# A state-space stage on one core: a gate copy, router scores and a residual placed later, and each convolution half made in two parts

## The reference

```
h  = layernorm(x) * (1 + ca) + sa
xs, z = split(h @ W_in.T)                       # 256 + 256 columns
xc = silu(conv over 4 rows (xs) + conv_b)       # one filter of 4 taps a column
dt, B, C = split(xc @ W_x.T, [64, 80])
dt = softplus(dt @ W_dt.T + b_dt)
h_t = exp(dt * A) * h_(t-1) + dt * B * xc       # 256 columns x 16 states
y  = sum over the 16 states of h * C, + D * xc
x  = x + ga * ((y * silu(z)) @ W_out.T)
h  = layernorm(x) * (1 + cb) + sb               # goes on to the router of the experts
```

## Time and profile before

| | us |
|---|---|
| median of 3 runs | 663.12 |
| the three runs | 655.6, 663.12, 663.97 |
| the profiled execution | 653.8 |
| its span in the trace | 651.7 |
| the loop over 64 steps, from the first scan to the last sum | about 32 to 277.5 |

### The profile page before, as it was taken

How to read it: one execution, slowest core, us unless ns; L and a number is a source line. 1 busy time by engine, 2 the same in 40 slices (tenths; PEclk the granted TensorE clock), 3 DMA queues, 4 the chain that set the end, 5 groups by cost and what they waited for, 6 DMA issues and landing times.

```text
span 651.7 us, 9201 instructions
## 1 busy us (share of the span) xinstructions
PE 511.0 (78%) x2287; PEld 314.1 (48%) x2287; DVE 454.8 (70%) x870; ACT 335.0 (51%) x667; POOL 426.0 (65%) x324
## 2 busy tenths in 40 slices
PE   8879969979997898977998882659887787847420
PEld 4324323423443333455998871225655676746320
DVE  5877989898989799874445531836780686668717
ACT  3757734674677354342333331563741787737605
POOL 2376989898899879703777775510107778777540
PEclk9779979997998968997999996998887899869675
DMA  6423335433223333012655553500026655452025
GB/s 200 129 77 122 134 129 172 138 102 115 97 97 108 115 89 112 13 41 85 184 182 169 159 139 97 197 2 0 17 76 189 209 165 162 131 134 87 32 86 140
DMA packets 47798, 75.47 MB, mean 116 GB/s; under 512 B 6434, under 2 KB 23716, under 8 KB 47620
## 3 DMA queue, kind: packets, MB, share of 16 engines
q1 hardware_dynamic: 42180, 63.48, 31.2%
q0 software_dynamic: 5568, 11.41, 6.7%
HBM read 65.76 MB, written 9.11 MB: 115 GB/s over the span
## 4 chain that ended last, share of the span: by engine, by line
PE 45%; DVE 18%; issue 10%; ACT 9%; POOL 7%; DMA 6%; DVEq 5%; SPq 1%; POOLq 0%
PE ps L1201 14%; PE ps L1164 4%; PE ps L1195 4%; DVE hs L1863 4%; DVEq L1929 4%; POOL y_dram L487 3%; PE ps L1509 3%; PE ps L1537 3%; PE ps L1400 3%; POOL xl L481 3%; DMA y_dram<-ys,rows_i 2%; PE ps L1108 2%; DVE freq L2070 1%; ACT ps L723 1%; DVE prod L1873 1%
## 5 line engine op out<-in xcount | busy, mean ns | idle before, releaser
L533 POOL TENSOR_TENSOR bu<-uT,b_sb 128x1024 f32<-128x1024 f32 x62 | 145.9, 2374 | 2.1 <-DMA b_sb<-b_rows 2.1
L1201 PE MATMUL ps<-prod,cst 128*128 128x512 f32 x256 | 130.2, 653 | 3.2 <-DVE yT L1883 3.2
L481 POOL DMA_INDIRECT xl<-h_dram,rows_i x87 | 87.6, 1007 | 62.0 <-DVE rows_i L1742 36.1
L487 POOL DMA_INDIRECT y_dram<-ys,rows_i x87 | 94.7, 1088 | 33.7 <-issue 23.5
L723 ACT ACTIVATE ps<-dtT,neg_a 128x512 f32<-128x512 f32 x128 | 85.2, 684 | 53.9 <-DVE hs L1863 53.5
L544 POOL TENSOR_TENSOR prod<-hs,c_sb 128x1024 f32<-128x1024 f32 x32 | 76.6, 2393 | 23.5 <-PE ps L1201 14.8
L1201 PEld LDWEIGHTS ps<-prod,cst 128*128 128x128 f32 x256 | 50.1, 206 | 82.8 <-issue 78.0
L1863 DVE TENSOR_TENSOR_SCAN hs<-ps,carry,bu 128x512 f32<-128x512 f32 x64 | 77.5, 1261 | 4.5 <-ACT ps L723 4.5
L1863 DVE TENSOR_TENSOR_SCAN hs<-ps,bu 128x512 f32<-128x512 f32 x64 | 73.9, 1203 | 7.3 <-ACT ps L723 7.1
L1509 PE MATMUL ps<-xt,mfr 128*128 128x128 f32 x384 | 56.3, 303 | 25.3 <-DVE freq L2062 15.9
L1509 PEld LDWEIGHTS ps<-xt,mfr 128*128 128x128 f32 x384 | 52.2, 215 | 28.1 <-issue 27.1
(11 more groups left out here) (289 smaller groups left out, 834.5 us busy)
## 6 DMA issues: line engine op xcount, KB each, us to landing
b_sb<-b_rows SPq DMA_DIRECT2D x31, 512.0 KB
mfr<-in_mf SPq DMA_DIRECT2D x48, 256.0 KB, 3.4
w1r<-in_w SPq DMA_DIRECT2D x39, 256.0 KB
c_sb<-b_rows SPq DMA_DIRECT2D x32, 256.0 KB, 3.5
w_s<-in_w SPq DMA_DIRECT2D x9, 256.0 KB, 3.9
h_dram<-h_tok SPq DMA_DIRECT2D x8, 256.0 KB
down_s<-in_down SPq DMA_DIRECT2D x1, 2048.0 KB, 9.9
xl<-h_dram,rows_i POOLq DMA_INDIRECT x87, 3.6
```

The lines of the kernel that those rows point to most:

```text
L481: pool.indirect_dma_start(xl[:, j % slots, :], None, h_dram[l], bass.IndirectOffsetOnAxis(ap=rows_i[:, 0, j:j + 1], axis=0)).then_inc(load ...
L487: pool.indirect_dma_start(y_dram[l], bass.IndirectOffsetOnAxis(ap=rows_i[:, 1, j:j + 1], axis=0), ys[:, j % XR, :], None).then_inc(saved[j ...
L533: nc.gpsimd.tensor_tensor(bu[:, g % RING, :, :], uT[:, c % 2, :, :], b_sb[:, k % BRING, g % 2, :].unsqueeze(1).broadcast_to([P, ND, CHUNK] ...
L1201: last = nc.tensor.matmul(bank(Y_BANK + d), ident, prod[:, g % RING, d, :], start=n == 0, stop=n == NS - 1)
```

## The change

The change has five parts. (1) PE: a convolution half no longer makes its four taps at once. Two stand where the four stood, then come the row of C and the sum of the even step, and then the other two; `conv_ps` is raised after the fourth. (2) ACT: the gate's second copy moves from n = 15 to n = 0 of the next chunk, behind the decays of that chunk's state 1. (3) DVE: the router scores are taken at n = 3 and not at 1, the residual is added at n = 7 and not at 6, its inverse deviation made at n = 10 and not at 9. (4) ACT: `rstd` at n = 9 and not at 8. (5) PE: 8 matmuls of `spin` ahead of the wait for the last chunk's columns, before the loop.

```diff
--- before.py
+++ after.py
@@ -757,8 +757,8 @@
                 nc.scalar.activation(ws[:, :, :, :].rearrange("p k b e -> p (k b e)"), src, ACT.Copy).then_inc(S["small_ready"], 1)
 
             before = {2: lambda c: conv_copy(c, 0), 4: lambda c: conv_copy(c, 1), 7: low_and_rows, 9: lambda c: dt_parts(c, 0),
-                      11: lambda c: dt_logs(c, 1), 13: lambda c: z_copy(c, 0), 15: lambda c: z_copy(c, 1)}
-            after = {8: lambda c: rstd(1, c), 12: normed_rows, 14: columns_out}
+                      11: lambda c: dt_logs(c, 1), 13: lambda c: z_copy(c, 0)}
+            after = {9: lambda c: rstd(1, c), 12: normed_rows, 14: columns_out}
             def mod_rows(lb):
 
                 m, src = mod[:, lb // BATCH, lb % BATCH, :, :], bank(MODB[lb]).rearrange("p (k c) -> p k c", c=C)
@@ -802,6 +802,8 @@
                     scaled_scores(vec[:, V["rw0"]], modT0, wq0)
                 if g == 6:
                     centred_scores(2, ps[:, BACK, 0:2 * BATCH * E0], ws0)
+                if n == 0 and c:
+                    z_copy(c, 1)
                 if n in before and c + 1 < NCHUNK:
                     before[n](c + 1)
                 if n == 5:
@@ -1153,17 +1155,19 @@
                 nc.tensor.matmul(bank(z_bank(c, d)), win_s[:, DIN + d * P:DIN + (d + 1) * P], hT[:, b, lo:lo + CHUNK],
                                  start=True, stop=True).then_inc(S["z_ps"], 1)
 
-            def conv(c, d):
-
-                pe.wait_ge(S["hT_sb"], c + 1)
-                pe.wait_ge(S["scaled"], 2)
-                if c:
-                    pe.wait_ge(S["z_raw"], 2 * c) if d == 0 else pe.wait_ge(S["xc_raw"], 2 * c + 1)
+            def conv(c, d, taps=range(TAPS)):
+
+                if taps[0] == 0:
+                    pe.wait_ge(S["hT_sb"], c + 1)
+                    pe.wait_ge(S["scaled"], 2)
+                    if c:
+                        pe.wait_ge(S["z_raw"], 2 * c) if d == 0 else pe.wait_ge(S["xc_raw"], 2 * c + 1)
                 b, lo = c // 2, c % 2 * CHUNK
-                for k in range(TAPS):
+                for k in taps:
                     last = nc.tensor.matmul(bank(conv_bank(c, d)), wconv[:, k, d * P:(d + 1) * P], hT[:, b, lo + k:lo + k + CHUNK],
                                             start=k == 0, stop=k == TAPS - 1)
-                last.then_inc(S["conv_ps"], 1)
+                if taps[-1] == TAPS - 1:
+                    last.then_inc(S["conv_ps"], 1)
 
             def low_rows(c):
 
@@ -1228,7 +1232,7 @@
                     last = nc.tensor.transpose(ps[:, BACK, t * P:(t + 1) * P], x_tok[:, c * CT + t, :], ident)
                 last.then_inc(S["hT_ps"], 1)
 
-            before = {0: lambda c: conv(c, 0), 1: lambda c: conv(c, 1), 3: low_rows, 4: lambda c: dt_rows(c, 0),
+            before = {0: lambda c: conv(c, 0, (0, 1)), 1: lambda c: conv(c, 1, (0, 1)), 3: low_rows, 4: lambda c: dt_rows(c, 0),
                       6: lambda c: z_half(c, 0), 7: lambda c: z_half(c, 1)}
             after = {2: project_out, 6: rows_back}
 
@@ -1253,6 +1257,8 @@
             transposes(2)
             b_row(1)
             transposes(3)
+            pe.wait_ge(S["dt_ready"], 1)
+            spin(FRONT, 8)
             pe.wait_ge(S["hT_sb"], 4)
             pe.wait_ge(S["scaled"], 3)
             c_row(0)
@@ -1281,6 +1287,8 @@
                 if m == 0 and c:
                     pe.wait_ge(S["y_ready"], c)
                 add_up(2 * k)
+                if m < 2 and c + 1 < NCHUNK:
+                    conv(c + 1, m, (2, 3))
                 if 0 < m < NS // 2 - 1:
                     pe.wait_ge(S["prod_pool"], k)
                     add_up(2 * k - 1)
@@ -1892,7 +1900,7 @@
 
 
             before = {11: lambda c: dt_and_u(c, 0), 12: lambda c: dt_and_u(c, 1)}
-            after = {2: gate_y, 6: add_x, 9: inverse_std, 15: router_rows}
+            after = {2: gate_y, 7: add_x, 10: inverse_std, 15: router_rows}
             first_dt(0)
             first_dt(1)
             first_inputs(0)
@@ -1902,7 +1910,7 @@
                 scans(g)
                 if g % 2:
                     products(g - 1)
-                if n == 1 and c >= 2:
+                if n == 3 and c >= 2:
                     take_logits(0, c - 2, c - 1, E0, BACK, ws0)
                 if n in before and c + 1 < NCHUNK:
                     before[n](c + 1)
```

## The result

| | before | after |
|---|---|---|
| median of 4 runs, us | 661.64 | 673.55 |
| the runs, us | 655.6 to 663.97 | 669.01 to 675.83 |
| profiled execution, its span, us | 653.8, 651.7 | 675.83, 673.8 |
| TensorE's mean granted clock | 0.880 | 0.879 |

The changed kernel takes 1.0248 of the time before (95% interval 1.02 to 1.0296): it is slower. The forecast had the sign and was too small: 665 was predicted, 2 us above the median then known, and the medians now lie 11.9 apart. (Executions of one kernel differ, and some come out a per cent or more longer than the rest; all ratios here leave those out.)

A forecast was written before the change was run, and what follows sets the result against it. POOL was near the bound, other idle times a ring of waits among engines. Chunks 0 to 3, 1.0 + 4.2 + 3.7 - 4.1 = +4.8 us on 653.8, gave 658.6; raised to the runs' level, 665, range 652 to 674.

The forecast's parts named there:

- The split's mechanism: Convolution in two parts: its halves end later, so ACT's copies and the decays DVE's scans need come later.
- T: Start of chunk 1: the time PE starts on the convolution, 102.05 us in the trace of before.
- the inverse deviation costs the same one step on: DVE, chunk 1: making the inverse deviation one step later leaves its cost unchanged, within the chunk's +4.2 us.
- Chunk 0: First chunk of the loop: split's 3.9 us against the spin's 2.5, less a 0.4 wait, for +1.0 us.
- The scan that waits at 59.45 starts later: DVE, chunk 0: the split moves the second half's end back 3.9 us; with the spin, the scan starts 1.4 later.
- the last rival: Much slower: PE idles more mid-chunk and loses its clock; two or three stretches add 7 to 11 us; chance 0.10.
- the spin, -2.5: PE before chunk 0: eight matmuls taking 3.6 us bring full clock earlier, gaining 2.5 us on C's row and gate halves.
- Chunk 3: Last chunk, no convolution to make: DVE waits of 5.1 us go, less about 1.0 for C's row; -4.1 us.
- The rule on locking out: DVE instructions with two SBUF inputs and GpSimd's lock each other out; applied to product u, range 4 us, no sign.
- The gate copy at nothing: Chunks 1 and 2: DVE's returned waits of 2.55 and 1.66 us are hidden by PE's late start, so cost nothing.
- Faster: Rival: returned waits count everywhere and the later convolution costs less; 652 to 657 us on the runs' level; chance 0.25.
- No change: Rival: holds in chunks 1 and 2 half as long, hidden by POOL's idle time; 661 on the runs' level; chance 0.15.

The follow-up runs named there:

- e1: The kernel before with only the convolution in two parts; 668.68 us, ratio 1.0166.
- e2: The changed kernel with its convolution halves whole again, all moves and the spin kept; runs from 656.3 to 671.97 us, no ratio on record.
- e6: The changed kernel with only the inverse deviation back at n = 9 and rstd at 8; ratio 1.0344 (second chip).
- e12: The changed kernel with the inverse deviation made by four instructions with one SBUF tensor each; 674.0 us, ratio 1.0166.
- e4: The kernel before with only scores at n = 3, residual at 7, inverse deviation at 10 and rstd at 9; 668.09 us, ratio 1.0174.
- e7: The kernel before with only the gate's second copy at n = 0 and the scores at n = 3; ratio 0.9924 (second chip).
- e11: The kernel before with gate copy and scores later and the inverse deviation in four instructions with one SBUF tensor each; 654.87 us, ratio 0.9857.
- e3: The kernel before with only the gate's second copy moved to n = 0 of the next chunk; 655.45 us, ratio 1.0002.

## Why the prediction was right and wrong

**The split's mechanism was right, its size in chunk 1 too.** By its own steps for chunk 1: copies at T + 6.5 and T + 13.95, measured T + 6.6 and T + 14.1. The scan of step 20 1.9 later, measured 2.5 (119.21 is T + 8.4, before T + 5.9). The scan of step 23 at T + 21.1, measured T + 21.4. The scan of step 24 at T + 26.5, measured T + 26.8. The wait of 0.9 inside the convolution is there three times at 0.87; this is the one of chunk 1:

```profile
118.28 1.96 PE L1167 MATMUL ps<-hT,wconv 128*128 128x512 f32 x4 [0.87 <-ACT xcT L675]
```

The residual costs the 1.92 us it was priced at: in e1, where it isn't moved, step 24 starts at T + 24.9. Chunk 1 came to +6.3 and not +4.2. T itself came 0.7 later after product 12 (16.1 us, before 15.4); "the inverse deviation costs the same one step on" was wrong already here, 1.42 us for 0.49; and the 0.5 subtracted for waits further on I found given back nowhere. Two slips of arithmetic there weigh 0.1 us at most (3.44 / 2 is 1.72; 4.6 less 0.5 is 4.1). Chunk 2, +4.3 for +3.7, is near.

**Chunk 0 is the step that failed most:** +1.0 predicted, +7.5 measured. Two terms of that sum are off. "The scan that waits at 59.45 starts later" by 3.9 for the split was right (e1: 4.1, counted from the row of C). The 0.4 wait behind it, at step 9, went too, as said. But a new one of 1.73 us came two steps on, at step 11, and the sum has nothing for it. PE had to wait for the product, 2.3 us idle, its clock fell, and eight sums took 5.40 us for 3.70. Behind them stood PE's rows for dt, which ACT waited for with the decays of step 11 behind that. PE, ACT and DVE in after:

```profile
69.83 1.12 PE L1199 MATMUL ps<-bc_f,sel_f 32*128 32x512 f32 x2 [2.30 <-DVE prod L1881]
70.88 5.40 PE L1205 MATMUL ps<-prod,cst 128*128 128x512 f32 x8
```

```profile
77.36 0.69 ACT L706 ACTIVATE dtT<-ps,vec 128x512 f32<-128x512 f32 x1 [2.88 <-PE ps L1192]
```

```profile
79.34 2.34 DVE L1871 TENSOR_TENSOR_SCAN hs<-ps,bu 128x512 f32<-128x512 f32 x2 [1.73 <-ACT ps L723]
```

With that the split comes to 5.3 where the sum had 3.5. Here the last rival, the clock lost in PE's new idle time, was partly right: 1.7 us once in chunk 0, and once more in chunk 1 (151.87, again 5.40), where I had two or three such stretches of 3.7 each. That its 675 us on the runs' level lies near the measured 673.55 is luck. The other term is the spin, -2.5. It rested on nine matmuls taking 4.02 us at the kernel's start, "so eight take 3.6". Those nine began from another state: in all four executions that have the eight, after, e2, e6 and e12, they took 1.89. They end 4.5 us too early and bring nothing: e2 and e6 have them and show chunk 0 as the kernels without (47.9 and 53.1, e1 53.2). The profiled execution of after had the clock late besides, +2.2, which e4 and e7 show to happen with no spin as well, and e2 and e6 not to happen with it. So chunk 0 is 5.3 of split and 2.2 of chance.

**Chunk 3: the step held, and its gain was eaten.** -4.1 was predicted. DVE's waits of 1.46 and for the scores are gone, as said, and e11, where nothing takes their place (the residual stays at n = 6 there), shows -4.3 (63.7 to 59.4). In after it is +3.2. The failed step is once more "the inverse deviation costs the same": 5.17 us where it had taken 1.06, and behind it a stretch to the last sums that is 3.2 longer, half of it by the same cause (e12). The rule on locking out was in the prediction, for the product u alone and as a spread with no sign; it was not asked of the other DVE instructions nearby that read two SBUF tensors. There are two, `ln_nmr` and the second one of the scores (`route`, 0.33 us in chunks 2 and 3 of before, 1.34 and 0.87 in after). That `ln_nmr` would take 5 us could not be read in the trace of before, where the longest was 1.06.

**The gate copy at nothing** in chunks 1 and 2 was right: e3 has 60.4 and 61.7 for 60.2 and 61.6.

**The levels.** The sum was +4.8 on the profiled execution, the medians show +11.9, the profiled pair +22. The measured 673.55 lies inside the range, under its top of 674, which the prediction gave to the clock rival; other terms took it there. The last compares one of the fastest executions before with the slowest after, in which the late clock has 2.2. The terms that the runs repeat, the split's 5.3, 3.3 and 2.5, the residual's 1.9 in two chunks and the 3.2 of chunk 3, make 18; the ratio of 1.0248 on 661.64 is 16.

**The rivals.** "Faster" fell: T came no earlier, and the decays came later. e11's 654.87 us lie in its range, but that is a kernel without the split and with another inverse deviation. "No change", the hold hidden by POOL's idle time, fell: POOL idled 45.2 us before products for 23.5.

## What to carry to other kernels

When a result is made later on one engine, look at the in-order engine that reads it and count what is queued behind that read: here two copies of 0.69 us held back the decays for every scan. Before you move work on an engine, list its small instructions that read two SBUF tensors beside a busy GpSimd: one of 0.16 us became 5 to 8 us here. A filler that is to keep the clock up has to reach the next work (a gap of 4.51 us lost it here, one of 0.62 did not), and its length is measured at the clock it will run at.

## What was unexpected of the hardware

A DVE product of two SBUF tensors with 128 x 4 elements, 0.13 to 2.36 us elsewhere in these traces, took 5.17 to 8.24 us in chunk 3 of seven kernels beside POOL instructions that follow each other without a pause, and ended each time within 0.1 us of the end of the last of them. At the ends of two or three POOL instructions inside that stretch it was not let in. In all other places where POOL was busy it was let in at the first such end, or in one case the second, with the next instruction right behind. What tells the two apart is open. With one SBUF tensor and a scalar column the same work took 0.55 to 0.58 us in four instructions, in every chunk.

The time at which the clock comes back varies, after the same 4.5 us of idle time too: in e2 and e6 within 6 us after PE takes up its work again, in after and e12 after some 11. That moved chunk 0 by 2.3 us.
